# Reordering additions, splits and LoRA merges at the ends of FFN phases, and dropping three no-operations of TensorE

## The reference

```
c   = cond(x)                       # x W^T + 2 * top-2-of-8 expert LoRA, rank 16
x   = x + attn(c)                   # 7 low-dimensional terms + (silu(c Wg^T) * (c Wu^T)) Wd^T, hidden 1248
d   = cond2(x)                      # x W^T + b + 2 * per-batch LoRA
h1  = d w1^T + 2 (d A1^T) B1^T      # FFN with LoRA on all three weights, hidden 1376
h3  = d w3^T + 2 (d A3^T) B3^T
x   = x + g w2^T + 2 (g A2^T) B2^T,     g = silu(h1) * h3
```

## Time and profile before

| | |
|---|---|
| median of 3 runs | 455.89 us (455.78 to 456.11) |
| profiled execution | 455.78 us, its span 454.1 us |
| PE busy | 448.8 us, 99% of the span, 2033 matmuls |
| DVE, ACT, POOL busy | 301.3 (66%), 196.2 (43%), 17.2 us (4%) |
| chain that ended last | PE 97%, DVE 2%, issue 1% |
| HBM traffic | 26.97 MB read, 2.10 MB written, 64 GB/s |

### The profile page before, as it was taken

How to read it: one execution, slowest core, us unless ns; L and a number is a source line. 1 busy time by engine, 2 the same in 40 slices (tenths; PEclk the granted TensorE clock), 3 DMA queues, 4 the chain that set the end, 5 groups by cost and what they waited for, 6 DMA issues and landing times.

```text
span 454.1 us, 5522 instructions
## 1 busy us (share of the span) xinstructions
PE 448.8 (99%) x2033; PEld 368.5 (81%) x2033; DVE 301.3 (66%) x455; ACT 196.2 (43%) x302; POOL 17.2 (4%) x37
## 2 busy tenths in 40 slices
PE   9999999999999999999999999999999999999997
PEld 7788888888887878887888888878878778888786
DVE  5756799677865356776676238988862567887631
ACT  6364442355563124655444437365541124664300
POOL 1004000240000000000000000000000000000000
PEclk9999999999999999999999999999999999999999
DMA  8406100122101321122530010222201122111022
GB/s 294 132 0 189 62 1 0 37 80 66 51 1 46 94 69 46 48 69 67 148 101 35 17 48 16 70 66 52 79 4 41 54 92 65 46 56 62 1 94 91
DMA packets 16266, 29.42 MB, mean 65 GB/s; under 512 B 2224, under 2 KB 2496, under 8 KB 16240
## 3 DMA queue, kind: packets, MB, share of 16 engines
q1 hardware_dynamic: 14976, 27.01, 18.9%
q0 software_dynamic: 1264, 2.07, 1.7%
HBM read 26.97 MB, written 2.10 MB: 64 GB/s over the span
## 4 chain that ended last, share of the span: by engine, by line
PE 97%; DVE 2%; issue 1%; ACT 0%; DVEq 0%
PE PS L1281 18%; PE PS L1282 18%; PE PS L1283 18%; PE PS L1418 13%; PE PS L1419 13%; PE PS L1420 13%; PE PS L1510 1%; PE PS L1344 1%; PE PS L1295 0%; PE PS L1569 0%; PE PS L1579 0%; PE PS L1580 0%; PE PS L1523 0%; PE PS L1293 0%; PE PS L1567 0%
## 5 line engine op out<-in xcount | busy, mean ns | idle before, releaser
L1418 PE MATMUL PS<-HT,WU 128*128 128x512 f32 x266 | 104.4, 392 | 1.4 <-PE PS L1283 0.6
L1419 PE MATMUL PS<-HT,WU 128*128 128x512 f32 x266 | 103.7, 390 | 0.0
L1420 PE MATMUL PS<-HT,WU 128*128 128x512 f32 x266 | 103.5, 389 | 0.0
L1418 PEld LDWEIGHTS PS<-HT,WU 128*128 128x128 f32 x266 | 49.9, 188 | 14.2 <-issue 1.4
L1420 PEld LDWEIGHTS PS<-HT,WU 128*128 128x128 f32 x266 | 49.9, 188 | 10.6
L1419 PEld LDWEIGHTS PS<-HT,WU 128*128 128x128 f32 x266 | 50.0, 188 | 10.0
L400 ACT ACTIVATE WU<-raw 128x256 fp32r<-128x256 f32 (+2 forms) x48 | 42.1, 884 | 26.2 <-DVE raw L948 8.7
L773 DVE TENSOR_TENSOR WU<-raw,WU 128x256 fp32r<-128x256 f32 (+2 forms) x49 | 48.5, 995 | 5.4 <-ACT WU L400 5.2
L400 ACT ACTIVATE PS<-PS 128x512 f32<-128x512 f32 x38 | 22.1, 582 | 67.1 <-PE PS L1420 67.0
L1282 PE MATMUL PS<-G,DW 128*128 128x512 f32 (+1 forms) x122 | 47.1, 386 | 0.0
L1281 PE MATMUL PS<-G,DW 128*128 128x512 f32 (+1 forms) x122 | 47.1, 386 | 0.0
(11 more groups left out here) (171 smaller groups left out, 681.6 us busy)
## 6 DMA issues: line engine op xcount, KB each, us to landing
raw<-in_pieces SPq DMA_DIRECT2D x87, 256.0 KB, 2.7
X<-in_x SPq DMA_DIRECT2D x8, 256.0 KB, 5.2
out_x<-X SPq DMA_DIRECT2D x7, 256.0 KB, 2.0
su_raw<-in_stk_up POOLq DMA_DIRECT2D x6, 192.0 KB, 2.6
T<-in_lora_b POOLq DMA_DIRECT2D x16, 32.0 KB, 2.1
ga_raw<-in_lora_a POOLq DMA_DIRECT2D x8, 32.0 KB, 3.1
out_x<-X SPq DMA_DIRECT2D x2, 128.0 KB, 1.7
sm<-in_small POOLq DMA_DIRECT2D x1, 95.5 KB, 3.5
```

What stands on the lines that cost most here:

```text
L1418: pe.matmul(bank, w[:, 1, cols], xx[:, 0, :], start=start and kc == 0, stop=False, skip_group_check=not start)
L1419: pe.matmul(bank, w[:, 0, cols], xx[:, 1, :], start=False, stop=False, skip_group_check=not start)
L1420: mm = pe.matmul(bank, w[:, 0, cols], xx[:, 0, :], start=False, stop=kc == 1, skip_group_check=not start)
```

## The change

Three kinds of edits; no instruction of the computation is added or taken away.

- PE no longer waits for its own pass and no longer issues the no-operation. ACT waits for `pass_done` where it waited for the `half_read` of that step, and the later counts of `half_read` are lower.
- In the first FFN, in the last chunk of each phase, the split of the first down-projection piece (`half_hi`, `half_lo`, `full_hi`, `full_lo` with index 0) moves from ahead of g's split to behind `copy_e` on ACT and behind `add_d` on DVE; `add_d` also moves ahead of `full_lo(0, 1)`.
- In the second FFN, `g_lo(1, 1)` moves from ahead of `su_lo(2)` to behind `add_d(1, 2)`, with a wait for it ahead of `mul1(1, 2)`; and `add_d` of the last chunk of each phase moves ahead of a LoRA merge (in the last chunk of all, ahead of a merge and a split).

```diff
@@ -504,8 +504,10 @@
 
             def half_hi(s, q):
 
-                if q >= 2:
-                    act.wait_ge(half_read, (0, 5)[s] + q - 1)
+                if s == 1 and q == 4:
+                    act.wait_ge(pass_done, 12)
+                elif q >= 2:
+                    act.wait_ge(half_read, (0, 4)[s] + q - (2 if q == 5 and s else 1))
                 p = P_HALF[s] + q
                 if s == 0:
                     act.wait_ge(raw_in[SLOT[p]], raw_count(p))
@@ -515,7 +517,7 @@
 
             def full_hi(s, j):
                 if j == 0:
-                    act.wait_ge(half_read, (5, 11)[s])
+                    act.wait_ge(pass_done, 8 * s + 8)
                 if j == 2:
                     act.wait_ge(p4_done, fast(s, (8, 9)[s]) + 1)
                 p = P_FULL[s] + j
@@ -596,9 +598,9 @@
             for c in range(1, 4):
                 steady(0, c)
             copy_bc(0, 4, g_mul[0], 4)
-            half_hi(0, 0)
             g_hi(0, 3)
             copy_e(0, 4)
+            half_hi(0, 0)
             fast_silu(0, 4, 0)
             half_hi(0, 1)
             fast_silu(0, 4, 1)
@@ -620,9 +622,9 @@
             for c in range(6, 9):
                 steady(0, c)
             copy_bc(0, 9, g_mul[0], 9)
-            full_hi(0, 0)
             g_hi(0, 8)
             copy_e(0, 9)
+            full_hi(0, 0)
             full_hi(0, 1)
             fast_silu(0, 9, 0)
             full_hi(0, 2)
@@ -1066,10 +1068,10 @@
                 steady(0, c)
                 mul1(0, c)
             mul0(0, 3)
-            half_lo(0, 0)
             g_lo(0, 3)
             add_b(0, 4)
             add_d(0, 4)
+            half_lo(0, 0)
             half_lo(0, 1)
             mul1(0, 4)
             mul0(0, 4)
@@ -1093,11 +1095,11 @@
                 steady(0, c)
                 mul1(0, c)
             mul0(0, 8)
-            full_lo(0, 0)
             g_lo(0, 8)
             add_b(0, 9)
+            add_d(0, 9)
+            full_lo(0, 0)
             full_lo(0, 1)
-            add_d(0, 9)
             full_lo(0, 2)
             mul1(0, 9)
             mul0(0, 9)
@@ -1195,15 +1197,16 @@
             classic_mul(1, 1)
             dve.wait_ge(t_made, 8)
             t_lo(T4, q2[B21], 8)
-            g_lo(1, 1)
 
             su_lo(2)
             sums(1, 3)
             part1_lo(1, 3)
             add_b(1, 2)
             add_d(1, 2)
+            g_lo(1, 1)
             part2_lo(1, 3)
             merge_chunk(4)
+            dve.wait_ge(g_ready, unit(1, 1) + 1)
             mul1(1, 2)
             for c in range(3, 5):
                 steady(1, c)
@@ -1216,8 +1219,8 @@
             half_lo(1, 0)
             g_lo(1, 4)
             add_b(1, 5)
+            add_d(1, 5)
             merge_half(1)
-            add_d(1, 5)
             half_lo(1, 1)
             mul1(1, 5)
             mul0(1, 5)
@@ -1258,9 +1261,9 @@
             full_lo(1, 0)
             g_lo(1, 9)
             add_b(1, 10)
+            add_d(1, 10)
             merge_full(2)
             full_lo(1, 1)
-            add_d(1, 10)
             merge_full(3)
             full_lo(1, 2)
             full_lo(1, 3)
@@ -1486,12 +1489,8 @@
                     mm = product(PB[bank], DW[:, n // 2 % 2], g_of(s, j, k % 2), slice(a, a + P), j == 0, j == count - 1)
                     if j == count - 1:
                         mm.then_inc(pass_done, 1)
-                if n % 2:
-                    if j == count - 1:
-                        pe.wait_ge(pass_done, 8 * s + 4 * ph + 4)
-                        pe.nop().then_inc(half_read, 1)
-                    else:
-                        mm.then_inc(half_read, 1)
+                if n % 2 and j != count - 1:
+                    mm.then_inc(half_read, 1)
 
             def down(s, h, j, done):
                 c0, n = PHASES[s][1]
```

## The result

The changed kernel takes 451.92 us (median of 6 runs, 451.75 to 452.37) against 456.00 us for the kernel before on the same chip (median of 6, 455.62 to 456.46). The ratio is 0.9915, 95% interval 0.9905 to 0.9925, so it is faster by about 4 us, 0.9%. The forecast was 452.1 us. The span of the profiled execution went from 454.1 to 450.2 us, and the profiled executions themselves took 455.78 and 451.92 us.

What follows compares the result with a forecast made beforehand. PE, busy 99% of the span, was taken as the bound. Parts 1 to 4, 1.51 + 0.59 + 0.62 + 1.09 = 3.81 us, came off 455.78 us, giving 451.97, with the median at 452.1 us; range 451.7 to 453.3.

Steps and rivals of the forecast that it cites:

- The eight stops: Places after the first 25 us where two PE starts lie further apart than the matmul rate allows; 3.81 us together.
- Part 1: Three no-operations, n=9 of the first FFN, n=5 and n=11 of the second: stops of 0.55, 0.40, 0.56 us go.
- The Trainium skill's rule: Matmul latency (398 + N)/2.4 ns: a wait exposes about 0.15 us, making the sum about 1.1 us smaller.
- rival 1: Behind the three passes only the drain goes, 0.16 us per stop; gain 2.79 us, time 453.1 us; chance 0.08.
- Part 2: Ends of the first FFN's phases: p3 waits for add_b, which comes earlier; stops of 0.29 and 0.30 us go.
- Part 3: Second FFN, ahead of chunk 3's p1: with g_lo(1, 1) moved, part 1 comes earlier and 0.62 us goes.
- Rival 2: Narrow covers of parts 2 and 3 (0.15, 0.25 us) fail, some stops stay; at worst 453.3 us; chance 0.13.
- Part 4: Ends of the second FFN's phases: add_d ahead of the merges, so p4's stops of 0.38 and 0.71 us go.
- Rivals 3 and 4: 3: the ring of weights becomes the bound, 459.1 us, chance 0.02. 4: waits replaced one for one, 455.9 us, chance 0.04.

Runs made afterwards that it cites:

- DVE's order old: The changed kernel with DVE's order at the first FFN's two phase ends as before, ACT's as changed; 455.07 us.
- waits on: The changed kernel with the three waits and no-operations of PE put back, so the new orders alone; 453.95 us.
- ACT's order old: The changed kernel with ACT's order at the first FFN's two phase ends as before, DVE's as changed; 453.08 us.
- g_lo first: The changed kernel with g_lo(1, 1) back ahead of su_lo(2) on DVE; 452.92 us.

## Why the prediction was right

- **The bound.** "Only what keeps PE from starting its next matmul can move the end" held. The eight stops were worth 3.81 us by the prediction's reading and 3.86 us by the second one, and the span fell by 3.86 us.
- **Part 1, 1.51 us.** Undone alone, 1.52 us (1.56 by the second reading). Right in size. In its reason it was right in that what is next in the queue was ready. But it said that the queue stands still until the last product is written; that is 1.0 us of it, and 0.5 us was the no-operation behind the wait. The forecast did not hang on this, since both went together.
- **The Trainium skill's rule and rival 1.** From the latency in the Trainium skill, TensorE: Matmul & The Clock Gate, section Single matmul latency, the prediction estimated about 0.15 us for a wait for the own product. The page gives that latency for a bf16 matmul and says nothing of a wait; the fp32r matmuls here are recorded at 0.39 us, close to its 0.379. The wait alone took 0.33 us in the run made for it, so the estimate was short by half: the drain is 0.16 us of it as estimated, and the 0.05 us to the next start and the 0.11 us of restart were left out. Rival 1 expected 1.02 us to stay behind the passes, and nothing stayed.
- **Part 2, 0.59 us.** Undone alone in ACT's half, 0.56 us (0.66 by the second reading). The chain of starts was right to 0.01 us, since each start followed from a distance that the trace had shown between the same two instructions.
- **Part 3, 0.62 us.** Undone alone, 0.59 us (0.62). The cover of p6, put at 0.48 us to its start (307.30 against 307.78), measured 0.49 us by making part 2 late. Rival 2, that the covers of parts 2 and 3 fail, did not come: PE has no stop at either place.
- **Part 4, 1.09 us.** Undone alone, 1.05 us (1.05). The late merges cost nothing.
- **Rivals 3 and 4.** The first piece's split starts at 138.31, 3.5 us later than before, as forecast, and ACT's copies in the down steps show no wait for a load; the ring did not become the bound. No stop came for one removed.

What was a little off: the time fell by 4.1 us and not by 3.8. Between the two profiled executions it fell by 3.86 us, all of it at the eight places, and the first 25 us gave 0.01 us. The other 0.2 us is between the profiled execution of the kernel before, 455.78 us, and its median of six, 456.00 us, so it is spread of the runs; that it came out on this side is luck.

## What to carry to other kernels

When the bounding engine shows as busy for 99% and more, read the distances between its starts and not its idle time: here eight stops lost 3.8 us and the table of waits named 1.3 us of it. Place the small copy or split that nobody waits for behind the one on the way to the bounding engine, on both engines that make it, since ACT's half of that edit without DVE's lost 2.7 us against the whole edit. And let another engine wait for a count that the last product gives, instead of letting TensorE wait for itself to pass the word on.

## What the runs showed of the hardware

A wait of TensorE for its own last product cost 0.32 to 0.34 us at three places, and a no-operation with its count behind it 0.07 to 0.25 us more; a no-operation without a wait cost nothing to be seen.

The first microseconds are the part that varies from run to run, and the traces show two sources. The first is TensorE's clock. PE starts with 39 small warm-up matmuls. In the changed kernel they are 0.107 us apart up to 4.2 us and 0.056 us from there. In the kernel with DVE's order old all are 0.107 us apart, and behind them the first four real matmuls are 0.57, 0.43, 0.42 and 0.43 us apart, where the changed kernel has 0.30, 0.24, 0.23 and 0.23. The trace's record of the granted clock begins at 4.22 us in the changed kernel and at 7.12 us in this one, just where the distances halve; in all twelve profiles it begins where they do, between 4.1 and 7.1 us. So before that point the clock stood at the lower of its two levels, 1.2 GHz, and behind it at 2.4 GHz. The table of stretches takes a time without a record for full clock: the last row below, from 5.20 to 7.20 us, reads 1.00 (third figure from the right) all the same.

The second source is a load. With the waits on and with ACT's order old, ACT waits 1.49 and 1.17 us for a small input, `sm`; its copies of `HT` come after that, and PE, whose weight loads then wait for DVE's `HT`, loses 0.5 us between 9 and 11 us. In the changed kernel ACT doesn't wait there. With g_lo first it waits 1.11 us, and PE loses 0.05 us.

Over the first 25 us the distances between starts lost 0.7 us in one profile and 1.5 us in another, a spread as large as most of the edits, so the times alone would not have told these apart. Rows of PE, the changed kernel and then DVE's order old; then ACT with the waits on; then the stretch of DVE's order old.

```profile
1.11 3.81 PE L1347 MATMUL PS<-warm 128*128 128x128 bf16 x39 [1.11 <-DVE warm L838]
```

```profile
1.11 4.34 PE L1347 MATMUL PS<-warm 128*128 128x128 bf16 x39 [1.11 <-DVE warm L838]
5.25 0.77 PE L1284 MATMUL PS<-HT,G 128*128 128x512 f32 x1
5.82 0.63 PE L1285 MATMUL PS<-HT,G 128*128 128x512 f32 x1
6.25 0.63 PE L1286 MATMUL PS<-HT,G 128*128 128x512 f32 x1
6.67 0.60 PE L1284 MATMUL PS<-HT,G 128*128 128x512 f32 x1
```

```profile
6.55 0.23 ACT L400 ACTIVATE WR<-sm 128x32 fp32r<-128x32 f32 x1 [1.49 <-DMA sm<-in_small]
```

```profile
5.20:7.20 2.00, 2.00 (x8) 1.59 (x6) 1.30 (x4) 1.26 (x2) 0.00 (x0) 1.00 0.97 334
```
